# Retention's rows, K tiles and quantised weights turned by transposing DMAs in place of TensorE

## The reference

```python
x = layernorm(x + attention(x))                      # causal, gated heads
q, k, v = x @ W_Q, ctx @ W_K, ctx @ W_V              # per head
q, k = xpos(q), xpos(k, downscale=True)              # x * cos + swapped(x) * sin
ret = ((q @ k.T) * decay_mask) @ v                   # retention, causal decay per head
ret = (ret - mean) / sqrt(var + 1e-5)                # per head
x = layernorm(x + (ret * silu(x @ g_w.T + g_b)) @ out_w.T + out_b)
xq = fake_quant(x)                                   # one scale for all of x
h = fake_quant(silu(xq @ wq(w_gate).T) * (xq @ wq(w_up).T))
x = layernorm(x + h @ wq(w_down).T)                  # wq: rounded to 8 bits, one scale per row
```

## Time and profile before

| what | value |
|---|---|
| median of three runs | 1857.51 us |
| profiled execution, first to last instruction | 1854.0 us |
| PE busy | 1693.4 us, 91% |
| DVE busy | 1387.5 us, 75% |
| ACT, POOL busy | 1049.5 us, 1042.0 us |
| retention phase | about 980 to 1582 us |

### The profile page before, as it was taken

How to read it: one execution, slowest core, us unless ns; L and a number is a source line. 1 busy time by engine, 2 the same in 40 slices (tenths; PEclk the granted TensorE clock), 3 DMA queues, 4 the chain that set the end, 5 groups by cost and what they waited for, 6 DMA issues and landing times. The chain is left out here.

```text
span 1854.0 us, 37186 instructions
## 1 busy us (share of the span) xinstructions
PE 1693.4 (91%) x13426; PEld 763.6 (41%) x13426; DVE 1387.5 (75%) x3039; ACT 1049.5 (57%) x1861; POOL 1042.0 (56%) x1001
## 2 busy tenths in 40 slices
PE   5998999999999999998787999999999998899996
PEld 2433344433433344333233455545455554444432
DVE  7687756777577856688744878878778777788798
ACT  5346555665556655566642556565465454555577
POOL 4049867677775976869872654555555555000044
PEclk9999999999999999999898999999999999899999
DMA  8302112231012311222224223232232131651265
GB/s 274 116 18 61 53 31 58 68 92 42 24 53 78 103 31 25 84 60 81 80 80 164 64 84 101 93 98 97 86 96 88 60 107 47 236 203 46 81 261 187
DMA packets 123039, 172.02 MB, mean 93 GB/s; under 512 B 22376, under 2 KB 73064, under 8 KB 121960
## 3 DMA queue, kind: packets, MB, share of 16 engines
q1 hardware_dynamic: 117336, 160.91, 27.0%
q10 hardware_dynamic: 5520, 8.73, 1.5%
HBM read 106.12 MB, written 38.14 MB: 78 GB/s over the span
## 5 line engine op out<-in xcount | busy, mean ns | idle before, releaser
L1148 DVE CUSTOM_DVE_ANT_0 a_mx<-a_mx,a_mqk 128x128 f32<-128x128 f32 (+3 forms) x512 | 242.0, 511 | 130.7 <-PE a_mx L1348 129.6
L960 ACT ACTIVATE a_P<-a_mx 128x512 f32<-128x512 f32 (+3 forms) x441 | 199.2, 496 | 150.7 <-PE a_mx L1366 80.4
L1231 POOL TENSOR_TENSOR a_P<-a_P 128x512 f32<-128x512 f32 (+3 forms) x202 | 194.2, 990 | 107.7 <-PE a_o L1378 94.6
L1362 PE MATMUL a_mx<-a_Qs,a_Ks 128*128 128x512 f16 (+3 forms) x768 | 231.3, 334 | 19.2 <-ACT a_P L960 7.5
L1348 PE MATMUL a_mx<-a_Ks,a_Qs 96*128 96x512 f16 (+3 forms) x768 | 226.3, 331 | 9.8 <-DVE a_nm L1148 3.0
L960 ACT ACTIVATE share<-a_mx 128x512 f32<-128x512 f32 (+3 forms) x327 | 144.9, 490 | 105.8 <-PE a_mx L1366 59.1
L1231 POOL TENSOR_TENSOR a_P<-a_P,share 128x512 f32<-128x512 f32 (+3 forms) x199 | 184.5, 957 | 27.2 <-ACT share L960 17.4
L1151 DVE TENSOR_REDUCE a_nm<-a_mx 128x1 f32<-128x512 f32 x256 | 164.8, 683 | 31.3 <-PE a_mx L1348 30.4
L2260 PE MATMUL r_pj<-share,cth 128*128 128x512 f16 x672 | 169.6, 386 | 3.6 <-PEq L123 2.7
L2260 PE MATMUL r_pj<-r_xTh,share 128*128 128x512 f16 x512 | 158.9, 383 | 4.4 <-DVE r_xTl L2106 3.7
L3008 PE MATMUL f_pj<-f_xqT,f_wgu 128*128 128x512 bf16 x704 | 158.6, 382 | 0.6 <-DVE f_xqT L2892 0.6
(11 more groups left out here) (302 smaller groups left out, 3999.9 us busy)
## 6 DMA issues: line engine op xcount, KB each, us to landing
x_scratch<-rows SPq DMA_DIRECT2D x60, 256.0 KB, 2.3
rows<-x_scratch SPq DMA_DIRECT2D x56, 256.0 KB, 4.5
lead<-in_xT SPq DMA_DIRECT2D x24, 512.0 KB, 4.4
lead<-in_ctxT SPq DMA_DIRECT2D x38, 256.0 KB, 2.8
h_scratch<-f_h SPq DMA_DIRECT2D x3, 2816.0 KB, 9.1
f_h<-h_scratch SPq DMA_DIRECT2D x3, 2816.0 KB, 9.8
a_Ks<-a_kph SPq DMA_DIRECT2D x256, 32.0 KB, 1.9
a_Qs<-a_qph SPq DMA_DIRECT2D x256, 32.0 KB, 1.9
```

Of the source, the lines that this page charges most:

```text
L960: act.activation(Pf[pf.at[key]][:, off:512], pb[:, off:512], ACT.Exp).then_inc(p_exp, 1)
L1148: dve.tensor_tensor_reduce(bank_of(it)[:, 0:n], bank_of(it)[:, 0:n], mqk[:, 512 - n:512], 1.0, -3e38, ALU.add, ALU.max, nm[:, col:col + 1] ...
L1231: pool.tensor_tensor(total[:, off:512], total[:, off:512], Pf[pf.at[key]][:, off:512], ALU.add).then_inc(add_pool, 1)
L1362: m = pe.matmul(pb[:, off:512], Ks[s][:, j, kt * P:(kt + 1) * P], Qs[s][:, j, qb * 512 + off:(qb + 1) * 512], start=True, stop=not diag)
```

## The change

K tiles, rows and quantised weights are turned by transposing DMAs, issued by SP, instead of by PE. For K and rows the order is reversed: the tile is split first, as it lies (rows in partitions), into the two halves of one float16 tile of 128x1024 (`ksp`, `xsp`, two of each), and one DMA turns high and low together. `kT` and `xT` hold both; of `xT` there are two sets, one for each half of a batch, so a half's turning waits for the last gate product of the half before the last. ACT's copy of the turned weights (`fcopy`) is gone: the DMA writes them into `fst`. POOL's K piece is cut in two pieces, `K` and `kd`. The planner counts 1.25 us on SP for each transposing DMA and 1.6 us more until it has landed.

```diff
 def k_out():
-    put("POOL", ("K", b, t), 2.45, k_pool, lambda: n < 2 or ... has(("Smm", n - 2)))
+    put("POOL", ("K", b, t), 1.23, k_sum)
+def k_sum():
+    put("POOL", ("kd", b, t), 1.23, lambda: done.add(("kd", n)), lambda: ... has(("Smm", n - 2)))
+    put("ACT", ("kt", b, t), 0.53, lambda: put("DVE", ("kt", b, t), 0.9, kt_split),
+        lambda: n < 2 or has(("kt", *divmod(n - 2, NT))))
+def kt_split():
+    done.add(("ktlo", n))
+    put("SP", ("kt", b, t), 1.25, lambda: after(1.6, kt_out), lambda: half_done(b - 1, t // 4))
...
-pe_item(KV, at_(6), ("kt", b, t), 1.0, kt_made, ...)
-pe_item(X, place, ("xT", *key), 1.0, made, ...)
 def rows(b, hf, k, place):
+    def landed():
+        put("ACT", ("xT", *key), 0.53, lambda: put("DVE", ("xT", *key), 0.9, split),
+            lambda: n < 2 or has(("xT", *HALVES[(n - 2) // 4], (n - 2) % 4)))
+    def split():
+        xrow.give(key)
+        put("SP", ("xt", *key), 1.25, lambda: after(1.6, lambda: done.add(("xT", *key))),
+            lambda: n < 8 or has(("Gmm", *HALVES[n // 4 - 2], 3)))
-    loads.append((place - 0.5 if n > 3 else -9.0, ...
+    loads.append((place - 0.9 if n > 3 else -9.0, ...
...
-put("ACT", ("fint", *key), 0.62, lambda: F.append((place, (("fturn", *key), 0.25, turned, ...
+put("ACT", ("fint", *key), 0.62, lambda: put("SP", ("fturn", *key), 1.25, lambda: after(1.6, turned)), ...
-    put("ACT", ("fcopy", *key), 0.6, copied)
...
 # SP
+kt:    w.wait_ge(kt_lo, n); w.wait_ge(r_mm, retained(b - 1, t // 4))
+       sp.dma_start_transpose(kT[:, :, t * P:(t + 1) * P], ksp[t % 2][:, :]).then_inc(kt_in[t % 2], 16)
+xt:    w.wait_ge(x_lo, n)
+       if h > 1: w.wait_ge(g_mm, num[("G", *HALVES[h - 2], 3)])
+       sp.dma_start_transpose(xT[h % 2][:, :, k * P:(k + 1) * P], xsp[k % 2][:, :]).then_inc(xt_in[k % 2], 16)
+fturn: w.wait_ge(fint_act, ...)
+       sp.dma_start_transpose(fst[...] as (p a b), fin[i][:, 0:wide]).then_inc(ft_in[i], 16)
-xT:    w.wait_ge(xt_mm, n - 2)
+xT:    w.wait_ge(x_lo, n - 2)
-fstore: w.wait_ge(fcopy_act, n)
+fstore: w.wait_ge(*int_turned(key))
 # ACT
-kt: w.wait_ge(kt_mm, n); w.wait_ge(r_mm, ...)
-    act.activation(kTh[...], bank[...], ACT.Copy)
+kt: w.wait_ge(k_pool, n); if n > 2: w.wait_ge(kt_in[t % 2], 16 * ((n - 1) // 2))
+    act.activation(ksp[t % 2][:, 0:D], m1[:, :], ACT.Copy)
-xT: w.wait_ge(xt_mm, n); w.wait_ge(g_mm, num[("G", *half_before(b, hf), 3)])
-    act.activation(xTh[...], bank[...], ACT.Copy, scale=XS)
+xT: w.wait_ge(xr_in[k % 2], 16 * ((n + 1) // 2)); if n > 2: w.wait_ge(xt_in[k % 2], 16 * ((n - 1) // 2))
+    act.activation(xsp[k % 2][:, 0:D], xrow[k % 2][:, :], ACT.Copy, scale=XS)
-fint: w.wait_ge(fturn_mm, num[("fturn", *fint.before[key])])
+fint: w.wait_ge(*int_turned(fint.before[key]))
-fcopy: act.activation(fst[...], bank[...], ACT.Copy)
 # DVE
-K:  w.wait_ge(kt_mm, n - 1)
+K:  w.wait_ge(kt_lo, n - 1)
-kt: dve.tensor_tensor(kTl[...], bank[...], kTh[...], ALU.subtract)
+kt: dve.tensor_tensor(ksp[t % 2][:, D:], m1[:, :], ksp[t % 2][:, 0:D], ALU.subtract)
-xT: dve.scalar_tensor_tensor(xTl[...], bank[...], XS, xTh[...], ALU.mult, ALU.subtract)
+xT: dve.scalar_tensor_tensor(xsp[k % 2][:, D:], xrow[k % 2][:, :], XS, xsp[k % 2][:, 0:D], ALU.mult, ALU.subtract)
 # PE
-fturn, kt, xT: four (or three) pe.transpose each
-Q, G: w.wait_ge(x_lo, num[("xT", b, hf, 3)])
+Q, G: for turned in rows_turned(4 * (2 * b + hf) + 4): w.wait_ge(*turned)
-A:  w.wait_ge(kt_lo, num[("kt", b, 4 * hf + 3)])
+A:  for turned in tiles_turned(b * NT + 4 * hf + 4): w.wait_ge(*turned)
```

## The result

| | before | changed |
|---|---|---|
| median of the runs | 1857.05 us | 1839.87 us |
| profiled execution, span | 1854.0 us | 1835.0 us |
| PE busy | 1693.4 us | 1659.4 us |
| DVE busy | 1387.5 us | 1402.5 us |

The ratio is 0.9906, 95% interval 0.9888 to 0.9924: some 17 us faster, where 36 were forecast. The same kernel in five more rounds took 1838.42 us, ratio 0.9904 (0.9889 to 0.9919).

The account below looks back on a forecast made before the run. PE was taken to set the pace in retention, DVE as second bound. A steady-part gain of 39 us less 3 at the start gave 36: span 1854 to 1818, forecast time 1821 us, range 1800 to 1840 (chance 0.55).

Parts of the forecast that it names:

- PE's term: Retention's steady part: removing the three transpose groups takes 48.3 us from PE's busy time, 459.6 to 411.3 us.
- My list: Signs of being right: transposes gone from PE, 2260's sums unchanged, stage some 36 us shorter, other stages within 2 us.
- The 10.5 us of waits: PE idle just ahead of K-tile and weight transposes (4.6 and 5.9 us), claimed to vanish with them.
- the steady part: Retention's window from 1030 to 1510 us; forecast to take 441 instead of 480 us, a gain of 39.
- The middle between a floor by PE and a ceiling by DVE: Steady part between 421 us (PE's need plus remaining idle) and 457 us (DVE 88% busy); 441 us taken.
- DVE's term: Steady part: both subtractions reading SBUF instead of PSUM add 13.9 us to DVE, ends -3 and +21 us.
- the rival with +21 us: DVE's subtractions cost more, both engines bind: steady part 465 us or more, time 1846 to 1857; chance 0.24 shared with SP.
- SP's term: SP's queue: 98 transposing DMAs, 1.25 us issue each (122 us) and 1.6 us more to land; room enough.
- the test I gave: Sign of being right: SP's transposes issued in about 1.25 us and landed by 3 to 4.
- The late case: Transposes land late, at ACT's weight casts and Q; slower from 7 us landing, 1892 us at 10; chance 0.17.
- Two signs that I gave for being wrong: PE idle before line 2260 released by the turned rows' DMAs; ACT idle before the weight cast on DMA.
- The start: First rows of retention, before the steady part: a longer chain through DMA, 3 us of loss taken (0 to 8).

## Why the prediction was right or wrong

**The direction and the range** held, the range by luck: 1839.87 us against an upper end of 1840, and three of the four other orders of the changed kernel took 1844 to 1855. Most of the prices held too. The size did not: 36 us forecast, 17 measured.

**PE's term was too large by 20 us: the step that failed first.** I took the groups' busy sums, 48.3 us, because a mean duration overlaps with its neighbours. But a group's sum overlaps with its neighbours of other groups too. What a piece holds PE for is the time from its start to that of the next piece, and the trace of before had it, in the timeline of PE (start, duration):

```profile
1114.97 0.39 PE L2284 MATMUL r_pj<-identb,r_fin 128*128 128x128 bf16 x4
1115.20 0.38 PE L2260 MATMUL r_pj<-share,r_zl 128*128 128x512 f16 x1
...
1116.06 0.60 PE L2289 MATMUL r_pj<-identf,lead 128*128 128x128 f32 x4
1116.50 0.59 PE L2260 MATMUL r_pj<-share,r_zh 128*128 128x512 f16 x2
```

0.44 us for a tile of four float32 transposes, whose duration reads 0.60, and 0.23 us for four of the weights, for 0.39. Some pieces hold PE longer than these two: read so for every one in the stretch before, idle time taken out, it is 13.9 us for K tiles, 14.7 for rows and 8.4 for weights, 37 us in all. That is 11 us below the group sums. PE's busy time fell by 28.0 us only, 9 less again, because the work that stayed on PE grew by 9: the context's products alone by 8.4 us from start to start. The low clock is worth some 6 of these 9 us, an estimate: PE was busy at it for 18.6 us of the changed stretch and 5.8 of the one before, and does half the work there. The rest has no cause shown. My list said "2260's sums unchanged"; the clock stood nowhere in the sum.

**The 10.5 us of waits did not vanish.** They were PE's waits ahead of the transposes. In the changed kernel others stand in their place, and PE idles 10.1 us more, not less. My sum allowed for that in its own way: 441 us with 411.3 busy was 29.7 us of idle, 9.3 more than before. By that the idle of the one changed kernel looks well forecast, and the miss (39 against 17.9 us in the steady part) is nearly PE's term alone. The orders show that this was luck. In the mean of five, idle rose by 19.0 us.

**The middle between a floor by PE and a ceiling by DVE was no estimate**, and was taken wrongly besides: between 421 and 457 lies 439, not 441. Both ends rested on an engine's sum. The runs show that the time follows neither: 25 us less on PE over the span, with the order kept, gave nothing, nor did 10 us less on DVE. PE at 93.7% of the stretch (476.06 of 508.30) is a chain of small waits in a fixed order, and those depend on that order.

**The order was no term at all.** I read in the code that the planner makes the orders and that the change alters its items, and I counted only the items. A new order alone moves this kernel by up to 12 us before and 17 us changed. That belongs into the range of every such forecast, and into the reading of the result.

**DVE's term was right.** 13.9 us forecast, +15.0 us over the span. The K subtraction took 868 ns for the 930 assumed, the rows' 977 for 919; by my sum (193 + 301) ns x 28 = 13.8 us. The context's scaled subtraction also grew, from 919 to 1104 ns, and the low part of q shrank, from 1195 to 1058 ns. So the rival with +21 us did not come. (Its time was summed wrongly: a gain of 15 us less up to 8 is 1842 to 1850 us, not 1846 to 1857.) DVE at 90% or more of the steady part, a sign that I gave for being right, did not come either: it is 441.8 of 508.3 us, 87%.

**SP's term was right in the issue, short in the landing.** 1.24, 1.26 and 1.20 us an issue against 1.25. From issue to landing 3.2 us for a K tile and 3.8 for rows, against 2.85; the test I gave (landed by 3 to 4) holds. The count of packets was right too: the DMA view of the stretch, before and changed, shows 77,025 more packets, where 83,000 were forecast for all 98 transfers, of which some fall before the stretch:

```profile
q1 hardware_dynamic: 36576, 44.71, 26.5%
```

```profile
q1 hardware_dynamic: 113601, 63.56, 51.4%
```

The price was not: I feared 60 ns for each, and the added ones took (0.514 x 508.3 - 0.265 x 526.2) x 16 / 77,025 = 25 ns. But I costed the lateness at nothing in the steady part and at 3 us at the start, and the kernel without these transfers was 9 us faster, by its profile 3.9 ahead of the first score matmul and 6.0 in the stretch.

What the data of one transfer take, its packets tell. Six of the K tiles' transfers had no other traffic beside them: 1,024 packets of 256 bytes and 32 of 4, the first 1.18 us after the issue began, the last done 1.41 to 1.43 us later, landed at 3.0 to 3.1 us. Seven plain loads of as many bytes of the context, alone too, went in 512 packets of 512 bytes and took 1.28 to 1.52 us.

The Trainium skill ("Advanced Engine Details and Errata", X-Bar Transpose) says that transposing DMAs are as fast as regular ones. That agrees with these 1.42 against 1.47 us (medians); the estimate of 0.7 us that I made from it doesn't, for the plain loads don't reach it either. The Trainium skill ("VectorE: DVE Perf Modes", The three transpose paths) gives 1309 ns for one block; my estimate of 10.5 us for eight in turn doesn't hold: the eight blocks of a K tile took 1.4 us together. That page's advice to prefer TensorE (its section Rules for kernel authors) is neither borne out nor refuted: over five orders each the kernel is 5.2 us the better by DMA, with a standard error of 4.1 at least.

**The late case did not come.** It needed a landing of 7 us; the medians are 3.2 and 3.8, and only one, the first K tile's, took longer than 7 (7.7). Two signs that I gave for being wrong did come, but small: ACT waited 12.3 us for the weights' landing, though nothing on PE waits for these weights any more, and PE waited 2.8 us for turned rows. **The start** took 1.1 us less than before, not 3 more; in the mean of five orders it is 68.2 us before and 68.3 changed from the last `a_o` matmul to the first score matmul. Without the transfers it is 63.1, so they add some 5 us there; what gives as much back isn't shown (PE's queue is free of the transposes there).

## What to carry to other kernels

Cost work on an engine by the time from its start to the start of what follows, not by durations or group sums, and then ask for evidence that the engine's time sets the pace: cut the work down in place, with the order kept, and see whether the time moves. Allow for the clock: here waits of PE were followed by stretches at half the clock, in which the work that stayed took longer. Where a planner or compiler makes the order, plan the same work several times with slightly different lengths before crediting a change with less than their scatter; here that scatter was 6 to 7 us for a result of 17. A busy share above 90% says that an engine is near the path, not that taking work from it shortens the path.

## What the runs showed of the hardware

- Transposing DMAs from SBUF to SBUF, 128x1024 two-byte values: 1.24 us of SP's queue for each and 3.2 to 3.8 us (median) from issue to landing; 128x512 or 128x384: 1.20 us, and 2.5 us to landing. They moved in packets of 256 bytes; the added ones took 25 ns each (18.85 MB more in 77,025 packets), where the packets of before, 1.2 KB in the mean, took 61 ns. With no other traffic beside it, the 256 KB of one took 1.42 us, as a plain load of 256 KB did (1.47).
- The granted TensorE clock fell to 1.2 GHz behind waits of PE, for 20.5 us of the changed stretch and 6.8 us of the one before; over five orders each it was 24.9 and 6.1 us. In such a place a matmul of 128x512 float16 took 632 ns, 380 elsewhere. Not every cluster of waits was followed by a fall: PE idled for 4 us in all between 1342 and 1351 us, and the clock stayed.
- Four float32 transposes of 128x128 held TensorE for 0.44 us from start to start (duration 0.60), four of bfloat16 for 0.23 (0.39).
- A DVE subtraction of 128x512 with both operands in SBUF took from 0.63 to 1.75 us (the K tile's: 627, 688 and 1750 ns), where the same from PSUM had a mean of 675.
- Attention, whose instructions are the same in all these kernels, ended between 957 and 965.3 us by the start of its last `a_o` matmul, and in three of the five changed orders at 963.9 to 965.3. I have no cause for it; in the one profiled execution of each it is 3.8 us of the difference of the means, against the change, which is why the stretch's 6.8 us is the better measure of what it does.
